# Dot products from two extra columns of a turning matmul, squares summed chunk by chunk, and one centring for both normalisations of a mixer

## The chip, the cores and the metric

The kernel runs on one core of a Trainium2 chip. A core has a matrix engine (TensorE, PE in the profile), a vector engine (VectorE, DVE), a scalar engine (ScalarE, ACT), GpSimd (POOL) and SyncE (SP, which here only issues DMAs). Each engine works through its own queue in order and waits on semaphores. The metric is the device time of one launch in microseconds (us).

## The reference

The input is 16 images of 48 channels, 64x64 pixels. Two layers, each a "mixer" and a small quantised feed-forward net, are applied with layer normalisation and residuals. The change touches the front of the second layer's mixer:

```python
center = x[:, :, H // 2, W // 2][:, :, None, None]
sim = (x * center).sum(1, keepdims=True) / (norm(center) * norm(x) + 1e-06)
x = x * (sim >= 0.7)
xd = einsum('hH,bcHW,wW->bchw', Mh, x, Mw)      # cosine transform over height and width
xt = xd.transpose(0, 2, 3, 1)
xn = (xt - xt.mean(-1)) / sqrt(xt.var(-1) + 1e-05) * ln_w + ln_b
# four quadrants of xn go through a state-space scan each; the result is added to xd,
# and the inverse transform follows
```

Before this, `x` is layer-normalised over its 48 channels: centred and scaled by 1/sqrt(var + 1e-6). So per pixel the mixer needs the sum of squares of the centred channels, their dot product with the centre pixel, a mask from both, the transform of the masked pixels, and a second normalisation over channels at each of the 64x64 frequencies.

## The kernel before

Images go in pairs: 2 x 48 channels fill 96 partitions, and the 4096 pixels lie along the free dimension. There are 8 pairs. Each engine's program is a prologue, a hardware loop over pairs 0 to 6 and a written-out last pair. At the loop's end the engine jumps back; pairs 1 to 6 begin behind such a jump, pair 0 comes straight from the prologue, pair 7 stands behind the loop.

One pair has these stages in the order of time:

- **The mixer's front.** With pixels on the 128 partitions (a "turned" tile is 32 groups of 128 pixels x 96 channels), VectorE finishes the sums of squares (line 1265) and dot products (1266), ScalarE takes logarithms and exponentials for the roots (920 to 926), VectorE forms the mask times 1/std (1271 to 1281) and scales the turned pixels (`scale(7, h)`, line 1258) in two halves. TensorE transforms columns (588, tile `pix`), turns back to rows (579), transforms rows (647); ScalarE evacuates each result from PSUM (888, 880). Then comes the second normalisation: VectorE sums channels, subtracts the mean (1252 to 1254), ScalarE squares (935), VectorE sums squares (1294), ScalarE takes ln and exp (937, 940), VectorE scales (1258 again), TensorE turns (579), ScalarE evacuates into `xq` (946).
- **The scan.** DMAs fetch `xq` back into shifted tiles, and 96 steps of multiply, scan and gather follow (lines 1323, 1328, 1417, 716, 735), with the first layer's convolution of a later pair woven in.
- **The inverse transform.**
- **The stream.** The feed-forward net of this pair, then the first net of the next pair ("ffn0"), then the normalisation ("norm") of the pair after that, chunk by chunk of 512 pixels. A norm step is: TensorE centres (538), ScalarE squares (860), TensorE averages (531), ScalarE takes ln and exp (849, 854), VectorE scales (1157) and sums (1160). Woven into the last steps is `turn_in`: for each of 8 chunks of 4 groups, TensorE turns the finished pixels of the next pair and centres them by the same matmul (514, the stationary operand is the pixels, the moving one the 96x96 matrix `centre`), and ScalarE copies the result to `pix` (836) and squares it into `pix2` (837).

The order is written by hand: `turned_in(parts, t)` says at which step t which chunk is turned. `take_centre` (1117 to 1120) picks up the centre pixel, broadcast to all partitions by a matmul with a selector (520); `sum_first_half` (1125 to 1130) multiplies the first 16 groups by it and sums both the products and the squares; GpSimd multiplies the other 16 groups (1388). `link` lets VectorE wait for its own last result. A small router for the convolution runs in the mixer's front too (1197 to 1231, TensorE 571, ScalarE 875).

Of the kernel before, what the change touches and what calls it, by code (L numbers as in the profile page):

```python
# [17 lines left out]
ALU = mybir.AluOpType  # L18
# [54 lines left out]
def program(nc, a):  # L73
# [9 lines left out]
    with ctx:  # L83

        ident = sb("ident", [128, 128])
        centre = sb("centre", [R, R])
# [40 lines left out]
        cb = sb("cb", [128, R])  # L127
        cb2 = sb("cb2", [128, R])
# [20 lines left out]
        pix2 = cut(128, GRP * R).rearrange("p (g r) -> p g r", g=GRP)  # L149
        sq = cut(R, LN_DEPTH * CH).rearrange("p (b n) -> p b n", b=LN_DEPTH)  # L150
# [52 lines left out]
        def two(b, rows=128):  # L203
# [44 lines left out]
        half_products = sem("half_products")  # L248
# [34 lines left out]
            (ident[:], "ident"), (centre[:], "centre"), (average[:], "average"),  # L283
# [28 lines left out]
        centre_ps = ps[:, 4, GB * R:(GB + 1) * R]  # L312
# [4 lines left out]
        (D_SUMS, D_MASKED, _, D_CENTRED2, _, D_VAR2, D_NORMED2, _) = range(1, 9)  # L317
        A_SQUARE = 1
        (A_LOG_V, A_LOG_S, A_RSTD, A_ROOT, A_SQUARE2, _, A_LOG2, A_RSTD2) = range(NG + 1, NG + 9)
        LN_DVE, LN_ACT = 8, NG + 8  # L320
        PROLOGUE, CHAIN = 27, 39
# [166 lines left out]
        def _(pe):  # L488
# [6 lines left out]

            def turn_in(P, n):

                c = IN_ORDER[n]
                if n == 0:
                    pe.wait_ge(hf_ready, P * 2 * NCH + NCH)  # L500
# [11 lines left out]
                for g in range(GB):  # L512
                    px = (c * GB + g) * 128
                    mm = pe.matmul(ps[:, 4 + n % 4, g * R:(g + 1) * R], x[:, px:px + 128], centre[:],
                                   start=True, stop=True)
                mm.then_inc(pix_ps, 1)
                if n == 1:

                    pe.wait_ge(ln_act, P * LN_ACT + A_SQUARE)
                    pe.matmul(centre_ps, sel_centre[:], pix[:, GRP // 2, :], start=True,  # L520
                              stop=True).then_inc(cen_ps, 1)

            def stream(n0, f0, parts, ready, src, P):

                for t in range(len(parts) + 3):
# [7 lines left out]
                    if t < len(parts):  # L533
# [4 lines left out]
                        pe.matmul(ps[0:R, j % LN_DEPTH, :], centre[:], src[parts[t]][:, j * CH:(j + 1) * CH],  # L538
# [26 lines left out]
                    if turned_in(parts, t) is not None:  # L565
                        turn_in(P, turned_in(parts, t))
# [256 lines left out]
        def _(act):  # L823
# [6 lines left out]
            chunk = lambda t, c: flat(t)[:, c * GB * R:(c + 1) * GB * R]  # L830

            def turn_in(P, n):
# [3 lines left out]
                act.activation(chunk(pix, c), ps[:, 4 + n % 4, 0:GB * R], ACT.Copy).then_inc(pix_act, 1)  # L836
                act.activation(chunk(pix2, c), ps[:, 4 + n % 4, 0:GB * R], ACT.Square).then_inc(ln_act, 1)

            def stream(n0, f0, parts, P):

                for t in range(len(parts) + 2):
# [27 lines left out]
                    if turned_in(parts, t) is not None:  # L869
                        turn_in(P, turned_in(parts, t))  # L870
# [42 lines left out]
            def pair(p, last):  # L913
# [4 lines left out]
                halves = lambda t: [flat(t)[:, h * GRP * R // 2:(h + 1) * GRP * R // 2] for h in range(2)]  # L918
# [17 lines left out]
                act.wait_ge(ln_dve, d0 + D_VAR2)  # L936
                act.activation(st[:, 2, :], st[:, 1, :], ACT.Ln, bias=eps[:, 1:2],
                               scale=1.0 / C).then_inc(ln_act, 1)
                act.wait_ge(ln_act, l0 + A_LOG2)
                act.activation(st[:, 3, :], st[:, 2, :], ACT.Exp, scale=-0.5).then_inc(ln_act, 1)  # L940
# [140 lines left out]
        def _(dve):  # L1081
# [20 lines left out]
            def link(ins):  # L1102
# [8 lines left out]
            sums_of_squares = lambda h: dve.reduce_sum(  # L1111
                nrm[:, 0, h * (ST // 2):(h + 1) * (ST // 2)], rows(half(pix2, h)), AXX)

# [448 lines left out]
```

## Time and profile before

| what | us |
|---|---|
| median of 3 runs | 4772.62 (4768.94 to 4777.07) |
| the profiled execution, its own time | 4770.02 |
| its span in the trace | 4768.1 |

| engine | busy us | share of the span |
|---|---|---|
| TensorE | 4072.2 | 85% |
| VectorE | 3633.8 | 76% |
| ScalarE | 2758.8 | 58% |
| GpSimd | 2337.8 | 49% |

The shares are means over unlike stages. In the scan nearly all engines are busy; in the mixer's front they take turns, and its time is that of the chain of waits through it. So the views below are of one pair, number 1, from the end of the stream before it (about 766 us) to the start of its scan (about 848 us).

### The profile page before, as it was taken

What the parts mean: (1) busy time and instruction counts of PE and PEld (TensorE: products, weight loads), DVE (VectorE), ACT (ScalarE), POOL (GpSimd) and SP (SyncE); (2) the same over time, 40 slices, a digit from 0 to 9 for tenths busy, and PEclk for the clock granted to TensorE, in tenths of its full rate; (3) what the DMA queues carried; (4) which work ended last, traced back from release to release, by engine and by line L of the source; (5) the groups of instructions that cost most, each with busy time, mean ns of one, the idle gap of its engine ahead of it and who ended that gap; (6) DMA issues with size and microseconds to landing.
All of it is one profiled execution on the core that took longest, in us unless ns stands there. A gap on an engine that the chain in (4) does not pass through costs nothing.

```text
span 4768.1 us, 49162 instructions
## 1 busy us (share of the span) xinstructions
PE 4072.2 (85%) x14248; PEld 1478.0 (31%) x14248; DVE 3633.8 (76%) x3157; ACT 2758.8 (58%) x3396; POOL 2337.8 (49%) x1084
## 2 busy tenths in 40 slices
PE   6779986899869998699986998779987799868997
PEld 2322233222332223322243222332233222332223
DVE  1469967699668996589965998659977699667996
ACT  2556646666566665566565664656647566565554
POOL 0137642476316773167631776227742477325663
PEclk9889988899889999799997998979999899887888
DMA  1147641577317762277623775247751576406661
GB/s 39 41 120 173 165 116 42 145 168 175 91 46 169 175 169 64 65 166 176 154 58 86 184 170 141 61 103 171 173 127 42 131 181 164 103 16 150 145 154 48
DMA packets 166829, 580.17 MB, mean 122 GB/s; under 512 B 22460, under 2 KB 23208, under 8 KB 162952
## 3 DMA queue, kind: packets, MB, share of 16 engines
q1 hardware_dynamic: 152168, 538.66, 47.4%
q10 hardware_dynamic: 14336, 37.76, 2.7%
q8 instruction: 132, 2.16, 0.2%
q14 instruction: 193, 1.58, 0.1%
HBM read 467.12 MB, written 71.48 MB: 113 GB/s over the span
## 4 chain that ended last, share of the span: by engine, by line
issue 32%; POOL 29%; PE 20%; ACT 9%; DVE 8%; DMA 1%; POOLq 0%; SPq 0%; ACTq 0%; DVEq 0%
POOL arena L1417 26%; PE ps L531 3%; PE ps L588 3%; ACT arena L867 2%; PE ps L670 2%; PE ps L579 2%; PE ps L735 2%; ACT arena L849 2%; POOL arena L1407 2%; DVE arena L1328 1%; PE ps L716 1%; PE ps L607 1%; POOL x L1425 1%; PE ps L561 1%; ACT arena L860 1%
## 5 line engine op out<-in xcount | busy, mean ns | idle before, releaser
L1417 POOL TENSOR_TENSOR arena<-arena 128x1024 f32<-128x1024 f32 x768 | 1859.6, 2421 | 972.1 <-DVE arena L1328 972.1
L1328 DVE TENSOR_TENSOR_SCAN arena<-arena,ps 128x1024 f32<-128x1024 f32 x768 | 1756.1, 2287 | 102.0 <-ACT arena L1020 4.5
L1020 ACT ACTIVATE arena<-arena,a_all 128x1024 f32<-128x1024 f32 x768 | 868.1, 1141 | 415.2 <-DVE arena L1328 277.3
L1323 DVE TENSOR_TENSOR ps<-ps,arena 128x1024 f32<-128x1024 f32 x768 | 930.7, 1212 | 159.1 <-PE ps L718 158.7
L716 PE MATMUL ps<-arena,spread 32*128 32x512 f32 x1536 | 905.0, 676 | 138.1 <-DVE arena L1328 87.3
L718 PE MATMUL ps<-arena,spread 32*128 32x512 f32 x1536 | 891.7, 676 | 0.0
L735 PE MATMUL ps<-arena,gather 128*32 128x512 f32 x3072 | 545.1, 656 | 41.2 <-POOL arena L1417 41.2
L781 PE MATMUL ps<-x 96*96 96x512 f32 x1008 | 498.5, 612 | 0.0
L716 PEld LDWEIGHTS ps<-arena,spread 32*128 32x128 f32 x1536 | 234.9, 191 | 782.0 <-issue 383.6
L670 PE MATMUL ps<-arena,w_in 96*96 96x512 f32 x512 | 322.5, 788 | 65.7 <-DMA arena<-xq 65.7
L1371 POOL TENSOR_TENSOR x<-x,arena 96x512 f32<-96x512 f32 x64 | 113.9, 1780 | 414.6 <-DVE arena L1180 414.6
L981 ACT ACTIVATE arena<-ps 128x512 f32<-128x512 f32 x128 | 76.4, 597 | 300.7 <-PE ps L702 300.7
L531 PE MATMUL ps<-arena,average 96*96 96x512 f32 x400 | 219.9, 632 | 30.8 <-ACT arena L860 30.8
L781 PEld LDWEIGHTS ps<-x 96*96 96x96 f32 x1008 | 143.1, 162 | 332.3 <-issue 332.3
L1305 DVE TENSOR_TENSOR arena<-arena 96x1024 f32<-96x1024 f32 x64 | 76.8, 1199 | 218.1 <-ACT arena L1006 218.1
L735 PEld LDWEIGHTS ps<-arena,gather 128*32 128x32 f32 x3072 | 107.9, 115 | 432.6 <-issue 354.3
L1407 POOL TENSOR_TENSOR arena<-arena 96x1024 f32<-96x1024 f32 x64 | 150.5, 2351 | 164.8 <-DVE arena L1305 164.8
L718 PEld LDWEIGHTS ps<-arena,spread 32*128 32x128 f32 x1536 | 229.8, 191 | 0.0
L1397 POOL MEMSET arena<- 96x6 f32 x8 | 0.8, 101 | 436.6 <-ACT xq L946 436.6
L849 ACT ACTIVATE arena<-ps,eps 96x512 f32<-96x512 f32 x200 | 136.4, 682 | 125.3 <-PE ps L531 125.3
L999 ACT ACTIVATE arena<-ps 96x512 f32<-96x512 f32 x128 | 70.7, 589 | 238.6 <-DVE arena L1313 226.8
L670 PEld LDWEIGHTS ps<-arena,w_in 96*96 96x96 f32 x512 | 103.3, 214 | 279.1 <-issue 210.3
(158 smaller groups left out, 5639.9 us busy)
## 6 DMA issues: line engine op xcount, KB each, us to landing
arena<-dl SPq DMA_DIRECT2D x768, 512.0 KB, 5.7
dl<-arena ACTq DMA_DIRECT2D x64, 384.0 KB, 6.2
x<-pn SPq DMA_DIRECT2D x56, 247.5 KB, 5.9
arena<-in_x SPq DMA_DIRECT2D x9, 1536.0 KB, 9.6
arena<-xq SPq DMA_DIRECT2D x64, 192.0 KB, 7.8
arena<-arena ACTq DMA_DIRECT2D x64, 192.0 KB, 5.6
out<-x SPq DMA_DIRECT2D x64, 192.0 KB, 2.1
arena<-xq SPq DMA_DIRECT2D x64, 191.8 KB, 6.7
```

Of the source, the lines that this page charges most:

```text
L531: pe.matmul(ps[0:R, LN_DEPTH + j % LN_DEPTH, :], average[:], sq[:, j % LN_DEPTH, :], start=True, stop=True).then_inc(averaged, 1)
L670: mm = pe.matmul(ps[0:DI, 6 + c, :], w_in[:, q, j, :], xs[:, i, c * 512 + 2 * j:c * 512 + 2 * j + 512], start=(j == 0), stop=(j == 1))
L716: pe.matmul(ps[:, bank, :], spread[rows[0], r, :], u[rows[0], i, 0:512], start=True, stop=True)
L718: pe.matmul(ps[:, bank + 1, :], spread[rows[1], r, :], u_low[rows[1], i, :], start=True, stop=True).then_inc(ubc_ready, 1)
L735: mm = pe.matmul(ps[b * BLK:(b + 1) * BLK, c, :], gather[:, r, :], hs[:, (r * TRIO + b) % HSS, c * 512:(c + 1) * 512], start=False, stop=( ...
L781: mm = pe.matmul(ps[0:R, 7, :], diag[:, k, :], taps_of(win[:, v % 2], k), start=(k == 0), stop=(k == TAPS - 1), skip_group_check=True)
L849: act.activation(lnv[:, k, :], ps[0:R, LN_DEPTH + k, :], ACT.Ln, bias=eps[0:R, e:e + 1]).then_inc(logged, 1)
L1020: act.activation(da[:, m % DAS, :], dbc[:, m % DBC, :], ACT.Exp, scale=a_all[:, v // 2, m:m + 1]).then_inc(da_ready, 1)
L1323: dve.tensor_tensor(driven, driven, bmat[:, v % 2, :], ALU.mult).then_inc(bu_ready, 1)
L1328: dve.tensor_tensor_scan(hs[:, m % HSS, :], da[:, m % DAS, :], driven, 0.0, ALU.mult, ALU.add).then_inc(h_ready, 1)
L1407: pool.tensor_tensor(u[:, i, :], delta, xi[:, i, :], ALU.mult).then_inc(u_ready, 1)
L1417: pool.tensor_tensor(product, product, cmat[:, v % 2, :], ALU.mult).then_inc(pr_ready, 1)
```

## The change

1. The moving matrix of the turning matmul becomes `turn_by`, 96x98: the 96 columns of `centre` and two more that hold the centred centre pixel of each image. One small matmul (`take_middle`) centres the centre pixel, and VectorE writes the two columns (`point_turn`). The dot products of all pixels then come out of the turning matmul as columns 96 and 97 of `turned`. Turning starts one step later, and ScalarE and TensorE run one step further. The products on VectorE and GpSimd and their sums go. The broadcast matmul has 2 columns in place of 96.
2. The squares are summed per chunk of 4 groups (`sum_squares`) in the stream's steps, the last chunk at the head of the pair's front.
3. The cosine transform acts on pixels, so channels that sum to zero before it sum to zero after it: the second subtraction of the mean goes. ScalarE squares the row transform straight from PSUM behind each copy; VectorE sums, and ln, exp and the scaling are done by halves.

```diff
@@ constants and tiles
-        centre = sb("centre", [R, R])
+        turn_by = sb("turn_by", [R, R + 2])
+        centre = turn_by[:, 0:R]
+        of_image = sb("of_image", [R, 2])
+        turned = cut(128, GRP * (R + 2)).rearrange("p (g r) -> p g r", g=GRP)
@@ def turned_in(parts, t):
-            return n if "ffn0" in parts and 0 <= n < NG else None
+            return n if "ffn0" in parts and 0 <= n <= NG else None
@@ TensorE
+            def take_middle(P):
+                pe.wait_ge(hf_ready, P * 2 * NCH + NCH)
+                settled(pe)
+                pe.wait_ge(ffn_done, P * 2 * NCH + MID // CH + 1)
+                pe.matmul(ps[0:R, 4, 0:2], centre, x[:, MID:MID + 2], start=True, stop=True).then_inc(centre_row, 1)
@@ def turn_in(P, n):
                 if n == 0:
-                    pe.wait_ge(hf_ready, P * 2 * NCH + NCH)
+                    pe.wait_ge(cvec_ready, P + 1)
-                    mm = pe.matmul(ps[:, 4 + n % 4, g * R:(g + 1) * R], x[:, px:px + 128], centre[:],
+                    mm = pe.matmul(ps[:, 4 + n % 4, g * TR:(g + 1) * TR], x[:, px:px + 128], turn_by[:],
-                    pe.matmul(centre_ps, sel_centre[:], pix[:, GRP // 2, :], start=True,
+                    pe.matmul(centre_ps, sel_centre[:], turned[:, GRP // 2, R:TR], start=True,
@@ ScalarE
-                evac(p, C_ROW, flat(xd[:]), 128, 512)
+                for c in range(NCR):
+                    act.wait_ge(pix_ps, p * PS_PAIR + ps_before(C_ROW) + c + 1)
+                    part = slice(c * 512, (c + 1) * 512)
+                    act.activation(flat(xd[:])[:, part], ps[:, c, :], ACT.Copy).then_inc(pix_act, 1)
+                    act.activation(flat(pix)[:, part], ps[:, c, :], ACT.Square).then_inc(ln_act, 1)
-                for h in range(2):
-                    act.wait_ge(ln_dve, d0 + D_CENTRED2 + h)
-                    act.activation(halves(pix2)[h], halves(pix)[h], ACT.Square).then_inc(ln_act, 1)
...
@@ VectorE, in the stream
+            def point_turn(P):
+                dve.wait_ge(centre_row, P + 1)
+                dve.tensor_tensor(turn_by[:, R:TR], ps[0:R, 4, 0:1].broadcast_to([R, 2]), of_image[:],
+                                  ALU.mult).then_inc(cvec_ready, 1)
+            def sum_squares(P, n):
+                c = IN_ORDER[n]
+                dve.wait_ge(ln_act, P * LN_ACT + A_SQUARE + n)
+                return dve.reduce_sum(nrm[:, 0, c * 2 * GB:(c + 1) * 2 * GB],
+                                      rows(pix2[:, c * GB:(c + 1) * GB, :]), AXX)
-                    if turned_in(parts, t) == 6:
-                        sum_first_half(P)
+                    if n == 0:
+                        point_turn(P)
+                    if n and n >= 2:
+                        sum_squares(P, n - 2)
+                    if n == 4:
+                        take_centre(P)
@@ VectorE, in the pair's front
-                dve.wait_ge(ln_act, a0 + NG)
-                sums_of_squares(1).then_inc(ln_dve, 1)
-                dve.wait_ge(half_products, (p + 1) * (NG // 2))
-                link(dve.reduce_sum(half_st(4, 1), rows(half(xd, 1)), AXX))
+                sum_squares(p, NG - 1).then_inc(ln_dve, 1)
...
-                    dve.wait_ge(pix_act, p * ACT_PAIR + act_before(C_ROW) + (h + 1) * NCR // 2)
-                    subtract_mean(xd, h)
-                for h in range(2):
-                    dve.wait_ge(ln_act, a0 + A_SQUARE2 + h)
-                    ins = dve.reduce_sum(half_st(1, h), rows(half(pix2, h)), AXX)
+                    dve.wait_ge(ln_act, a0 + A_SQUARE2 + (h + 1) * NCR // 2 - 1)
+                    dve.reduce_sum(half_st(1, h), rows(half(pix, h)), AXX).then_inc(ln_dve, 1)
                 for h in range(2):
-                    scale(3, h)
+                    dve.wait_ge(ln_act, a0 + A_LOG2 + 2 * h + 1)
+                    scale(xd[:], 3, h)
```

On VectorE, the end of the stream, the loop's jump and the head of a pair's front. Before (1157 and 1160 are a norm step's scaling and sum, 1111 a half's sum of squares, 1197 the router):

```order
L1157 TENSOR_TENSOR arena<-ps,arena 96x8x64
L1160 TENSOR_REDUCE chunk_sums<-arena 96x1
L1125 TENSOR_TENSOR xd<-arena,cb 128x1536
L1128 TENSOR_REDUCE st<-xd 128x32
L1111 TENSOR_REDUCE nrm<-arena 128x32
L1350 UNCONDITIONAL_BRANCH
L1197 TENSOR_REDUCE pooled<-chunk_sums 96x1
```

The same place after the change, where 1172 and 1175 are the norm step's two instructions and 1144 is a chunk's sum of squares:

```order
L1172 TENSOR_TENSOR arena<-ps,arena 96x8x64
L1175 TENSOR_REDUCE chunk_sums<-arena 96x1
L1144 TENSOR_REDUCE nrm<-arena 128x8 x3
L1358 UNCONDITIONAL_BRANCH
L1358 ISA
L1144 TENSOR_REDUCE nrm<-arena 128x8
L1215 TENSOR_REDUCE pooled<-chunk_sums 96x1
```

Three long instructions ahead of the jump became three short ones, and the two long ones behind it (1111 and 1266) became one short one.

On VectorE, the second normalisation before, from the end of the router (1231) to the first scaling (1258):

```order
L1231 TENSOR_TENSOR x<-ident,sel_small 96x864
L1290 ISA
L1252 TENSOR_REDUCE st<-xd 128x32
L1106 REGISTER_ALU
L1253 TENSOR_SCALAR st<-st 128x32
L1106 REGISTER_ALU
L1254 TENSOR_TENSOR arena<-xd,st 128x1536
L1290 REGISTER_ALU
L1252 TENSOR_REDUCE st<-xd 128x32
...
L1254 TENSOR_TENSOR arena<-xd,st 128x1536
L1293 REGISTER_ALU
L1294 TENSOR_REDUCE st<-arena 128x32
```

And after, where 1303 is a half's sum of squares and 1271 the scaling:

```order
L1249 TENSOR_TENSOR x<-ident,sel_small 96x864
L1302 REGISTER_ALU
L1303 TENSOR_REDUCE st<-arena 128x32
L1302 REGISTER_ALU
L1303 TENSOR_REDUCE st<-arena 128x32
L1305 REGISTER_ALU
L1271 TENSOR_TENSOR arena<-xd,st 128x1536
```

Six instructions of VectorE ahead of the sums of squares are gone. On ScalarE the six evacuations of the row transform now alternate with six squares (949 is the copy, 950 the square):

```order
L947 REGISTER_ALU
L949 ACTIVATE xd<-ps 128x512
L950 ACTIVATE arena<-ps 128x512
L947 REGISTER_ALU
L949 ACTIVATE xd<-ps 128x512
L950 ACTIVATE arena<-ps 128x512
```

Before, six copies stood there alone, and two squares of 1536 columns (935) followed them behind waits for VectorE.

## Rows read from the trace of the kernel before

**Rows 1.** Windows of pair 1: us; PE, PEld, DVE, ACT, POOL busy; PEclk; DMA; GB/s
```profile
786.00:803.00 17.00, 0.71 (x3) 0.62 (x4) 14.55 (x21) 1.47 (x6) 1.27 (x2) 0.55 0.32 102
820.00:833.00 13.00, 1.83 (x5) 0.52 (x3) 12.16 (x9) 5.36 (x7) 0.00 (x0) 0.70 0.00 0
```

**Rows 2.** Chain of waits, same pair: start us, us, what
```profile
827.27 3.42 DVE st L1294 x2
```

**Rows 3.** Timeline, VectorE, stream's end and front: start, us, what, [idle before]
```profile
785.63 0.68 DVE L1160 TENSOR_REDUCE chunk_sums<-arena 96x1 f32<-96x512 f32 x1
786.44 2.44 DVE L1125 TENSOR_TENSOR xd<-arena,cb 128x1536 f32<-128x1536 f32 x1
788.92 1.75 DVE L1128 TENSOR_REDUCE st<-xd 128x32 f32<-128x1536 f32 x1
790.79 1.75 DVE L1111 TENSOR_REDUCE nrm<-arena 128x32 f32<-128x1536 f32 x1
794.20 0.16 DVE L1197 TENSOR_REDUCE pooled<-chunk_sums 96x1 f32<-96x8 f32 x1 [1.66 <-issue]
794.58 1.74 DVE L1111 TENSOR_REDUCE nrm<-arena 128x32 f32<-128x1536 f32 x1
796.24 1.74 DVE L1266 TENSOR_REDUCE st<-xd 128x32 f32<-128x1536 f32 x1
798.58 0.23 DVE L1271 TENSOR_TENSOR nrm<-nrm 128x66 f32<-128x66 f32 x1
```

**Rows 4.** Timeline, ScalarE, same place
```profile
785.89 0.49 ACT L837 ACTIVATE arena<-ps 128x384 f32<-128x384 f32 x1
796.36 0.35 ACT L920 ACTIVATE nrm<-nrm,eps 128x66 f32<-128x66 f32 x1 [9.98 <-DVE nrm L1111]
...
796.91 0.24 ACT L926 ACTIVATE nrm<-nrm 128x66 f32<-128x66 f32 x1
```

**Rows 5.** Timeline, TensorE, same place
```profile
783.33 1.92 PE L514 MATMUL ps<-centre,x 96*128 96x96 f32 x16
794.72 0.48 PE L571 MATMUL ps<-router_w,pool_lhs 96*96 96x4 f32 x2 [9.47 <-DVE pool_lhs L1198]
```

**Rows 6.** Timeline, VectorE, prologue: the router's sum behind TensorE's product
```profile
66.64 0.16 DVE L1204 TENSOR_TENSOR rt<-ps,router_b 96x4 f32<-96x4 f32 x1 [0.58 <-PE ps L571]
```

**Rows 7.** Timeline, GpSimd, stream's end
```profile
785.32 1.95 POOL L1388 TENSOR_TENSOR xd<-arena,cb 128x384 f32<-128x384 f32 x2 [1.52 <-ACT arena L836]
```

**Rows 8.** Timeline, one norm step of the stream: TensorE, ScalarE, VectorE
```profile
779.38 1.10 PE L531 MATMUL ps<-arena,average 96*96 96x512 f32 x2 [0.19 <-ACT arena L860]
...
780.51 0.68 ACT L849 ACTIVATE arena<-ps,eps 96x512 f32<-96x512 f32 x1 [0.42 <-PE ps L531]
781.89 0.69 DVE L1157 TENSOR_TENSOR arena<-ps,arena 96x512 f32<-96x512 f32 x1 [1.61 <-ACT arena L854]
782.39 1.10 PE L531 MATMUL ps<-arena,average 96*96 96x512 f32 x2 [0.19 <-ACT arena L860]
```

**Rows 9.** Timeline, ScalarE, the row transform's evacuation
```profile
817.57 0.60 ACT L880 ACTIVATE xd<-ps 128x512 f32<-128x512 f32 x1
818.43 0.60 ACT L880 ACTIVATE xd<-ps 128x512 f32<-128x512 f32 x1 [0.26 <-PE ps L647]
```

**Rows 10.** Timeline, VectorE, the second normalisation
```profile
819.92 1.75 DVE L1252 TENSOR_REDUCE st<-xd 128x32 f32<-128x1536 f32 x1 [9.57 <-ACT xd L880]
827.27 3.40 DVE L1294 TENSOR_REDUCE st<-arena 128x32 f32<-128x1536 f32 x2
831.38 3.43 DVE L1258 TENSOR_TENSOR arena<-arena,st 128x1536 f32<-128x1536 f32 x2 [0.70 <-ACT st L940]
```

**Rows 11.** The first instruction after the front, GpSimd: min/median/max ns, first and last start
```profile
L1397 POOL MEMSET arena<- x8: 101/101/102, 262.5 to 4283.6; 96x6 f32 x8
```

**Rows 12.** The same line in windows of pairs 3 and 4
```profile
L1397 POOL MEMSET arena<- x1: 101/101/101, 1989.6 to 1989.6; 96x6 f32 x1
...
L1397 POOL MEMSET arena<- x1: 101/101/101, 2571.0 to 2571.0; 96x6 f32 x1
```

More of the change, by code:

```diff
@@ L282, in program @@
         loads = [
-            (ident[:], "ident"), (centre[:], "centre"), (average[:], "average"),
+            (ident[:], "ident"), (centre, "centre"), (of_image[:], "of_image"), (average[:], "average"),
             (pool_mask[:], "pool_mask"), (dct_t[:], "dct_t"), (dct_i[:], "dct_i"),
@@ L311, in program @@
         IN_ORDER = (NG // 2,) + tuple(c for c in range(NG) if c != NG // 2)
-        centre_ps = ps[:, 4, GB * R:(GB + 1) * R]
+        TR = R + 2
+        MID = (H // 2) * W + W // 2
+        centre_ps = ps[:, 4, GB * TR:GB * TR + 2]
         logits = ps[0:R, 2, GB * R:GB * R + E]
-        (D_SUMS, D_MASKED, _, D_CENTRED2, _, D_VAR2, D_NORMED2, _) = range(1, 9)
+        D_SUMS, D_MASKED, D_VAR2, D_NORMED2 = 1, 2, 4, 6
         A_SQUARE = 1
-        (A_LOG_V, A_LOG_S, A_RSTD, A_ROOT, A_SQUARE2, _, A_LOG2, A_RSTD2) = range(NG + 1, NG + 9)
-        LN_DVE, LN_ACT = 8, NG + 8
-        PROLOGUE, CHAIN = 27, 39
+        A_LOG_V, A_LOG_S, A_RSTD, A_ROOT = range(NG + 1, NG + 5)
+        A_SQUARE2, A_LOG2 = NG + 5, NG + 5 + NCR
+        LN_DVE, LN_ACT = 7, A_LOG2 + 3
+        PROLOGUE, CHAIN = 24, 31
         XSL = 16 * 2
@@ L537, in stream @@
                             pe.wait_ge(normed, n - LN_DEPTH + 1)
-                        pe.matmul(ps[0:R, j % LN_DEPTH, :], centre[:], src[parts[t]][:, j * CH:(j + 1) * CH],
+                        pe.matmul(ps[0:R, j % LN_DEPTH, :], centre, src[parts[t]][:, j * CH:(j + 1) * CH],
                                   start=True, stop=True).then_inc(centred, 1)
@@ L564, in stream @@
                         mm.then_inc(fc2_ready, 1)
-                    if turned_in(parts, t) is not None:
-                        turn_in(P, turned_in(parts, t))
+                    n = turned_in(parts, t)
+                    if n == 0:
+                        take_middle(P)
+                    if n:
+                        turn_in(P, n - 1)
             def router(count):
@@ L835, in turn_in @@
                 act.wait_ge(pix_ps, P * PS_PAIR + ps_before(T_IN) + n + 1)
-                act.activation(chunk(pix, c), ps[:, 4 + n % 4, 0:GB * R], ACT.Copy).then_inc(pix_act, 1)
-                act.activation(chunk(pix2, c), ps[:, 4 + n % 4, 0:GB * R], ACT.Square).then_inc(ln_act, 1)
+                bank = ps[:, 4 + n % 4, 0:GB * TR]
+                act.activation(flat(turned)[:, c * GB * TR:(c + 1) * GB * TR], bank, ACT.Copy).then_inc(pix_act, 1)
+                act.activation(pix2[:, c * GB:(c + 1) * GB, :],
+                               bank.rearrange("p (g r) -> p g r", g=GB)[:, :, 0:R],
+                               ACT.Square).then_inc(ln_act, 1)
             def stream(n0, f0, parts, P):
-                for t in range(len(parts) + 2):
+                for t in range(len(parts) + 3):
                     if 0 <= t - 1 < len(parts):
@@ L868, in stream @@
                                        ACT.Copy).then_inc(hf_ready, 1)
-                    if turned_in(parts, t) is not None:
-                        turn_in(P, turned_in(parts, t))
+                    if turned_in(parts, t):
+                        turn_in(P, turned_in(parts, t) - 1)
             def router(count):
@@ L1283, in pair @@
                 for h in range(2):
-                    scale(7, h)
+                    scale(turned[:, :, 0:R], 7, h)
                 if not last:
@@ L1468, in constants @@
         "ident": np.eye(128, dtype=np.float32),
+        "of_image": same[:, 0:R:C],
         "centre": np.eye(R, dtype=np.float32) - same / np.float32(C),
```

62 lines of the change are left out of this document (18 added, 44 removed).

## The prediction, made before the changed kernel was run

> **What bounds the kernel now.** I read four views, in this order. The windows first: in the 17 us behind the stream's end VectorE is busy for 14.55 us and TensorE for 0.71 us, and in the 13 us of the second normalisation VectorE for 12.16 and TensorE for 1.83 [rows 1]. So in these two stretches one engine works and the rest wait. The chain of waits next: it says whether that engine's work sets the end. It lies on VectorE there, with the two sums of squares of the second normalisation as one piece of 3.42 us [rows 2]. Then the timelines of VectorE and of the engines that wait for it: ScalarE has been idle for 9.98 us when it may take its first logarithm [rows 4], TensorE for 9.47 us before the router's product [rows 5]. Last the idle times inside one norm step of the stream, since the change adds work there. The step is 3.01 us long (782.39 - 779.38), and each engine has room in it: TensorE 0.19 us, ScalarE 0.42, VectorE 1.61 [rows 8]. The stream's own bound is the loop square, average, ln, exp, next square, and it stays.
>
> All of the change lies between the last norm step and the mixer's evacuation, a stretch in which nothing overlaps with another pair. Every microsecond that leaves VectorE's chain there leaves the pair's period, and there are 8 pairs.
>
> **The stream.** Turning starts one step later. In the step where it began, 8 matmul instructions (16 take 1.92 us, so about 0.9) leave TensorE's queue, and the centre pixel's product comes in, which has the form of the router's 96x4 product, 0.48 us [rows 5]. The stream ends about 0.4 us earlier. From the next step on a step holds what it held. The 98 columns in place of 96 cost 2% of 0.9 us, 0.02 us, inside TensorE's 0.19. ScalarE copies 392 columns in place of 384, 0.01 us inside 0.42. VectorE gets a sum of 384 columns in the later steps. Its price: 512 columns take 0.68 us and 1536 take 1.75 [rows 3], so 1.045 ns a column, and 384 take 0.55 us; it fits into 1.61. The centre's pick-up (three small instructions before, one now) comes one step later, ahead of the bank that the fifth turning reuses; I count nothing, since it also sheds two instructions. VectorE's small write of the two columns (about 0.2 us, by the 0.23 us of line 1271 [rows 3]) waits for TensorE's product. Behind it in VectorE's queue is only the feed-forward net's cast, which is needed a step later, so again nothing.
>
> **The end of the stream and the front's head (pair 1).** Before, the last norm sum starts at 785.63 and the root chain (line 1271) at 798.58: 12.95 us [rows 3]. In them lie 1125 (2.44), 1128, two 1111 and 1266 (1.75 each), 9.4 us of work, the router's small pieces, and 1.66 us of idle time at the loop's jump.
> After: the norm sum starts at 785.26 (0.37 earlier). The first of the three short sums follows 0.81 us behind, as 1125 did, at 786.07. They follow each other every 0.47 us (the duration less 0.08, as 1266 starts 1.66 us behind an 1111 of 1.74), so the third starts at 787.01 and ends at 787.56. ScalarE's squares keep ahead: its last one began at 785.89 [rows 4]; it has one chunk more behind the last norm step (0.75 us) and starts 0.37 earlier, so it is through by 786.8.
> Then the jump. Line 1197 starts 1.66 us behind the end of the last instruction ahead of the jump and 3.41 behind its start [rows 3]. The trace doesn't tell which counts, and short instructions hide less of it. From the end, the eighth sum starts at 789.22; from the start, at 790.42. I take the middle, 789.8, since both readings come from one row, and keep 0.6 us either way.
> Behind it: 1197 at 790.27, the router's product 0.52 us later (794.72 - 794.20) [rows 3, 5], 0.48 us long, VectorE's answer at about 791.3 (in the prologue it idled 0.58 us there, where nothing hid the product [rows 6]), and line 1271 about 0.5 us on, at 791.8. ScalarE's four roots take 0.79 us (796.36 to 797.15) [rows 4] behind the sum's end at 790.35: 791.2, so the router is now what is late, by 0.6 us. Before, it was hidden by 1111 and 1266.
> Gain: 798.58 - 791.8 = 6.8 us in the six pairs behind a jump. In pairs 0 and 7 no jump stands there: 787.48 for the eighth sum, 1271 at 789.5, against 796.8 before (798.58 less the jump's 1.75), 7.3 us. Together 6 x 6.8 + 2 x 7.3 = 55.4 us.
> From 1271 to the first scaling the same eight small instructions run; one reads two columns of `turned` with a step, 64 elements, and I count nothing.
>
> **The scaling of the turned pixels.** It reads `turned` with a row of 98 and writes `pix`, 1536 columns. Two took 3.43 us, 1.75 for the first [rows 10]. The nearest dear row is 1125, also 1536 columns with a broadcast operand: 2.44 us. That instruction began while GpSimd's product ran, until 787.27 (785.32 + 1.95) [rows 7], and 787.27 + 1.6 is its end, 788.88 [rows 3]. I take 1.75; 2.44 stays as the upper end, 0.7 us for the first half of either scaling, 1.4 us a pair, 11 us in all.
> The Trainium skill, "SBUF — State Buffer", section "SBUF: two separate sides", has it that VectorE and GpSimd share a port pair that is locked for a whole instruction, whichever starts first. By that rule the 2.44 has its cause in GpSimd, which does nothing in the new front, and the upper end falls away: 11 us less at the top of the range. This trace agrees in the one place where it can be seen.
>
> **The second normalisation.** Before: the first copy of the row transform starts at 817.57 and the copies follow every 0.86 us, paced by TensorE, with ScalarE idle for 0.26 [rows 9]. VectorE's chain runs from 819.92 to the scaling at 831.38 [rows 10], 13.81 us behind the first copy.
> After: copy and square per chunk. Back to back, copies overlap by about 0.1 us (line 837's kind is started every 0.38 us at 0.48 long; I use 0.50 for 0.60), so a chunk takes 1.0 us, more than TensorE's 0.86: ScalarE sets the pace, not TensorE. The sixth square ends 6.1 us behind the first copy, at 823.67; the third has ended at 820.67, and VectorE sums that half from there, then the other from 823.7 to 825.45. The scaling of half 0 follows at 825.4; its ln and exp (32 columns, at most 0.6 us) ran on ScalarE from 823.7 on. Gain 831.38 - 825.4 = 6.0 us. The other half's ln and exp lie beside that scaling. Bounds: 0.86 us a chunk if the squares hid wholly, 1.20 if nothing overlapped: -0.7 to +1.0 us a pair.
> 8 x 6.0 = 48 us.
>
> **Sum.** 55.4 + 48 = 103.4 us off the profiled execution's own 4770.02 us: 4666.6. The median of the runs stands 2.6 us above that execution, so 4669. One more small load among 28 at the start costs under 1 us. TensorE's clock is at its lower level for most of the front (0.55 granted [rows 1]) and I leave it so; behind shorter waits it might be higher, which I don't price.
>
> **Rivals.**
> *The jump holds the front back.* If the stretch without instructions is tied to something earlier than the last sum (the sequencer reaches the jump early, and what it waits for comes when it comes), the first instruction behind it stays at 794.20 - 0.37, so the eighth sum is 4.0 us later than in my sum, in six pairs: +24 us, 4693. The same holds if ScalarE's or TensorE's jump is longer than VectorE's; before, their 9.98 and 9.47 us of idle time hid it [rows 4, 5]. For it: 3.41 us is long for a jump. Against: VectorE's own restart lies behind its last instruction as far as can be read. Chance 0.10.
> The Trainium skill, "Runtime: NRT & Kernel Launch", section "Instruction fetch mechanics", says that a taken branch outside the fetched pages stalls the engine until the target is fetched. By this rule every engine pays at the jump, whatever work it has left, and this rival is the form it would take here. The 1.66 us agree with it; its size on ScalarE and TensorE this trace can't show.
> *ScalarE and the scalings are dearer.* At 1.20 us a chunk and 2.44 us for a scaling: +8 + 11 = +19 us, 4688. For it: line 1125. Against: line 1258 and GpSimd's row. Chance 0.08.
> *The turning outgrows its step.* This is the slower side. If a product of 98 columns, written at a step that is no multiple of 96, cost what half of a 512-column product costs (0.5 us, as the pieces of line 531 [rows 8]) in place of 0.12, a chunk's 8 pieces would take 3 us more, 2.8 beyond TensorE's room, in 8 chunks: +22.7 us a pair, +182 in all, 4851, slower by 1.6%. It decides from 103 / 64 = 1.6 us beyond the room per chunk. Nothing in the profile speaks for it. Chance 0.03.
> That the front isn't on the path after all would leave no change; the chain contradicts it. Chance 0.01.
>
> **How the numbers follow.** The forecast has 0.78. Its own range: the jump 6 x 0.6 = 4 us either way, ScalarE's pace -6 to +8, and the pairs themselves. The last differ for equal work: from pair 3 to pair 4 it is 581.4 us [rows 12], and the mean over seven is (4283.6 - 262.5) / 7 = 574.4 [rows 11]. For that I add 7 us either way. 4652 to 4688, stretched to 4691 towards the first two rivals. A measurement of this kernel tells about 0.2% (9.5 us) from no change. Faster: 0.78 + 0.10 + 0.08 = 0.96; same 0.01; slower 0.03.
>
> **What would show it.** In the changed profile: no GpSimd work between its last residual sum and the memset; three sums of 0.55 us ahead of the jump and one behind; line 1282 (the old 1271) 6 to 7 us earlier behind the last norm sum; norm steps still 3.01 us long; copy and square in pairs of 1.0 us with no wait for TensorE; the scaling some 7.8 us behind the first copy in place of 13.8; a scan as long as before. I'd be wrong if ScalarE's first logarithm waited for its own queue and not for VectorE, if the step of the stream grew, or if the scan took back what the front gives.

## The result: 78 us faster, 25 less than forecast

| | before | changed | ratio (95% interval) |
|---|---|---|---|
| median, us | 4771.73 (4768.94 to 4777.07, 4 runs) | 4694.1 (4684.73 to 4708.91, 4 runs) | 0.9839 (0.9811 to 0.9867) |
| profiled execution: own time / span, us | 4770.02 / 4768.1 | 4697.47 / 4695.7 | |

The forecast was 4669 with a range of 4652 to 4691: 25 us too low, and the measured median lies 3 us outside the range. The first rival, "the jump holds the front back", had been priced at 4693; how much that is worth is said below.

The page of the changed kernel, part 1 (busy us, share of the span, instructions):

```profile
span 4695.7 us, 49142 instructions
PE 4071.1 (87%) x14264; PEld 1475.5 (31%) x14264; DVE 3527.9 (75%) x3125; ACT 2758.9 (59%) x3444; POOL 2307.8 (49%) x1052
```

VectorE has lost 106 us of work and GpSimd 30; ScalarE and TensorE have what they had. The span fell by 72 us. So where did the path not shrink with VectorE's work? The timeline of VectorE at the front of pair 1 of the changed kernel shows it (start, us, what, [idle before]); the rows answer to [rows 3] and [rows 10]:

```profile
767.02 0.68 DVE L1175 TENSOR_REDUCE chunk_sums<-arena 96x1 f32<-96x512 f32 x1
767.82 1.47 DVE L1144 TENSOR_REDUCE nrm<-arena 128x8 f32<-128x384 f32 x3
775.64 0.55 DVE L1144 TENSOR_REDUCE nrm<-arena 128x8 f32<-128x384 f32 x1 [6.35 <-issue]
...
777.14 0.16 DVE L1222 TENSOR_TENSOR rt<-ps,router_b 96x4 f32<-96x4 f32 x1 [0.57 <-PE ps L586]
777.62 0.23 DVE L1282 TENSOR_TENSOR nrm<-nrm 128x66 f32<-128x66 f32 x1
...
780.20 3.43 DVE L1271 TENSOR_TENSOR arena<-arena,st 128x1536 f32<-128x1536 f32 x2
...
799.46 1.75 DVE L1303 TENSOR_REDUCE st<-arena 128x32 f32<-128x1536 f32 x1 [9.86 <-ACT arena L950]
...
804.06 3.42 DVE L1271 TENSOR_TENSOR arena<-xd,st 128x1536 f32<-128x1536 f32 x2
```

In this stretch one number is far from the forecast. The three short sums end at 769.29, the loop's jump follows, and VectorE's next instruction starts at 775.64: 6.35 us with nothing to do, where [rows 3] had 1.66. "issue" means that the engine waited for nothing that the profile shows. The chain of waits has the same hole on the path (start, us, what):

```profile
769.29 6.24 issue
```

ScalarE and TensorE wait for VectorE over this time, as in [rows 4, 5], and TensorE's norm step is still 3.02 us long (763.78 - 760.76, [rows 8]):

```profile
776.23 0.35 ACT L935 ACTIVATE nrm<-nrm,eps 128x66 f32<-128x66 f32 x1 [7.69 <-DVE nrm L1144]
```

```profile
760.76 1.10 PE L543 MATMUL ps<-arena,average 96*96 96x512 f32 x2 [0.19 <-ACT arena L876]
...
763.78 1.10 PE L543 MATMUL ps<-arena,average 96*96 96x512 f32 x2 [0.19 <-ACT arena L876]
...
776.62 0.48 PE L586 MATMUL ps<-router_w,pool_lhs 96*96 96x4 f32 x2 [9.09 <-DVE pool_lhs L1216]
```

What else begins at 767? The queue of SyncE (start, us to issue, what):

```profile
767.01 0.31 SPq L458 DMA_DIRECT2D pn<-arena  x1
```

This is the store of the normalised image, 1.6 MB. It waits for the scaling of the last norm step (line 1172, the semaphore `normed`), and so goes out as the last norm sum begins. The view of DMA by queue tells what the DMA engines did in the first 5 us behind the jump, and in the 3 us after that (queue, kind: packets, MB, share of the 16 engines):

```profile
DMA packets 86, 1.34 MB, mean 268 GB/s; under 512 B 9, under 2 KB 9, under 8 KB 9
q1 hardware_dynamic: 86, 1.34, 85.2%
```

```profile
q1 hardware_dynamic: 10, 0.05, 4.7%
q14 instruction: 4, 0.03, 3.3%
q8 instruction: 1, 0.02, 1.9%
```

From 768.2 to 773.2 only the store's packets move. Packets of the kind "instruction" come between 773.2 and 776.2, when the store has all but drained, and VectorE restarts then. I read them as the code behind the jump; the experiments below test that. Before, the store was issued at 785.62 and the jump, by the trace's record of the branch, came at 790.89. (A branch's record lies ahead of the end of the work already handed over: here the long sum ran on to 792.54.) The store, then the DMA queues from 790.9 to 792.0 and from 792.0 to 794.2:

```profile
785.62 0.31 SPq L453 DMA_DIRECT2D pn<-arena  x1
```

```profile
q1 hardware_dynamic: 18, 0.17, 42.1%
```

```profile
q1 hardware_dynamic: 7, 0.03, 3.9%
q8 instruction: 1, 0.02, 2.6%
q14 instruction: 2, 0.02, 2.0%
```

So only 0.20 MB of the store was left at the jump, and the first of the two packets of queue 14 started 1.2 us behind it. Now the jump comes at 768.13, 1.1 us behind the store, and the first such packet 5.3 us behind the jump.

Added up over the eight pairs of the two profiled executions, in us from start to start (the root chain begins with line 1271, now 1282; the first copy is that of the row transform, the second scaling that of the second normalisation):

| stretch | before | changed | difference | forecast |
|---|---|---|---|---|
| last scan to last norm sum (7) | 867.0 | 864.3 | -2.7 | -2.6 (0.37 each) |
| last norm sum to root chain | 99.9 | 72.0 | -27.9 | -52.4 |
| root chain to first copy of the row transform | 149.1 | 151.7 | +2.6 | 0 |
| first copy to second scaling | 110.4 | 61.5 | -48.9 | -48 |
| second scaling to first scan | 333.8 | 335.6 | +1.8 | 0 |
| the scans | 2921.1 | 2921.3 | +0.2 | 0 |

The start up to the first norm sum took 2.0 us more and the end behind the last scan 0.4, which with the rows makes the 72.4 us of the span. In the second row the six pairs behind a jump went from 12.9 to 13.3 us to 10.6 to 11.0; pairs 0 and 7, with no jump there, from 11.1 and 10.3 to 3.9 and 3.6.

### The profile page after: what moved, and what is told of

The parts are those of the page before. It is cut to its first block, busy times and chain, and to the rows that moved or that the text cites. A ratio compares the mean times of both kernels' runs of the same rounds, so it can differ in the third digit from the quotient of the medians.

```text
span 4695.7 us, 49142 instructions
## 1 busy us (share of the span) xinstructions
PE 4071.1 (87%) x14264; PEld 1475.5 (31%) x14264; DVE 3527.9 (75%) x3125; ACT 2758.9 (59%) x3444; POOL 2307.8 (49%) x1052
## 4 chain that ended last, share of the span: by engine, by line
issue 33%; POOL 30%; PE 18%; ACT 10%; DVE 7%; DMA 1%; POOLq 1%; SPq 0%; ACTq 0%; DVEq 0%
POOL arena L1416 27%; PE ps L543 3%; PE ps L603 3%; DVE arena L1336 2%; ACT arena L883 2%; ACT arena L865 2%; PE ps L594 2%; POOL arena L1406 2%; PE ps L750 2%; PE ps L685 1%; PE ps L622 1%; POOL x L1424 1%; ACT arena L876 1%; PE ps L731 1%; PE ps L573 1%
## 5 line engine op out<-in xcount | busy, mean ns | idle before, releaser
L685 PE MATMUL ps<-arena,w_in 96*96 96x512 f32 x512 | 311.9, 765 | 68.1 <-DMA arena<-xq 68.1
```

Of the source, the lines that this page charges most:

```text
L685: mm = pe.matmul(ps[0:DI, 6 + c, :], w_in[:, q, j, :], xs[:, i, c * 512 + 2 * j:c * 512 + 2 * j + 512], start=(j == 0), stop=(j == 1))
```

## The experiments

The kernel before ran on the chip beside each group of runs: 4766.57 us beside e1 to e4, 4766.54 beside e5 to e8, 4765.24 beside e9 and e10.

Theory A: the code behind the jump is fetched by the same DMA engines as the store, and waits for the store's packets that are already in flight. The rivals are given with each run.

**The store later.** In the changed kernel the store waits until ScalarE has written the logarithms, which come behind the jump:

```diff
                     sync.dma_start(a["xsp"], x[:]).then_inc(x_spilled, 16)
+                    sync.wait_ge(ln_act, p * LN_ACT + A_LOG_V)
+                    settled(sync)
                     sync.wait_ge(normed, p * LN_PAIR + LN_FIRST)
                     sync.dma_start(a["pn"], padded).then_inc(pn_out, 16)
```

> The changed kernel, with the store of the normalised image (pn, 1.6 MB) issued behind ScalarE's first logarithm of the pair's front, so behind the loop's jump, and no longer right behind the last norm step. Theory A (the instructions of the loop's head are fetched by DMA, and that fetch stands behind the store): VectorE's idle time at the jump falls from 6.35 us to 1 to 2 us, the norm sum to root chain (lines 1175 to 1282) from 10.6 to 5.5 to 6.5 us in six pairs, 26 to 30 us in all: about 4665 us. Theory B (the restart is tied to something earlier in VectorE's own queue, or the jump costs a fixed time): the idle time stays at 6.3 us, about 4694 us.

Measured: 4666.51 us (4662.93 to 4679.3, 5 runs), ratio 0.9795 (0.9769 to 0.9821). VectorE of this run, the store, and the DMA queues from 768.2 to 772.2:

```profile
767.10 0.68 DVE L1177 TENSOR_REDUCE chunk_sums<-arena 96x1 f32<-96x512 f32 x1
...
771.35 0.55 DVE L1146 TENSOR_REDUCE nrm<-arena 128x8 f32<-128x384 f32 x1 [1.97 <-issue]
```

```profile
772.44 0.31 SPq L460 DMA_DIRECT2D pn<-arena  x1
```

```profile
q14 instruction: 4, 0.03, 3.0%
q8 instruction: 1, 0.02, 2.0%
```

The code now comes at once, the idle time is 1.75 to 1.97 us, and from the last norm sum to the root chain it takes 6.0 to 6.2 us; the sum over the pairs is 44.1 for 72.0. 28 us came back with one wait, more than the 24.5 us that this row lacked of the forecast, and with them the total is within 3 us of the forecast's 4669. Theory B (a fixed time, or one tied to VectorE's own queue) falls: nothing of VectorE's changed. The store in front of the jump is the whole of what the forecast missed.

**The same wait in the kernel before.**

> The kernel before with the same later store. Theory A: its idle time of 1.66 us at the jump falls below 1 us, since the long sum ahead of the jump hides most of an undisturbed fetch: 4 to 9 us in all, about 4765 us. Theory B: 1.66 us and 4772 us.

Measured: 4769.9 us (4759.73 to 4775.48, 10 runs), ratio 1.0003 (0.9988 to 1.0017). The idle time at the jump fell from 1.65 to 2.03 us to 1.20 to 1.49:

```profile
787.99 0.16 DVE L1199 TENSOR_REDUCE pooled<-chunk_sums 96x1 f32<-96x8 f32 x1 [1.27 <-issue]
```

That is 2.4 us in all, less than the 4 to 9 us of the expectation, and the idle time did not fall below 1 us; in the total nothing is seen. The long work before the jump had given the store time to drain. So the store cost 0.4 us a pair before and 4.6 us after, in the six pairs behind a jump: the change made it dear by making VectorE early.

**A second store behind the first.** The changed kernel, and the same 1.6 MB once more to a buffer that nobody reads:

```diff
                     sync.dma_start(a["pn"], padded).then_inc(pn_out, 16)
+                    sync.dma_start(a["pn2"], padded).then_inc(pn_out, 16)
```

> The changed kernel with a second store of the same 1.6 MB, to another tensor, right behind the first. Theory A: the fetch waits for both, some 6 us more at each of six jumps (12 us idle in place of 6.35), about 4730 us. Theory B: 4694 us and 6.3 us.

Measured: 4690.63 us (4683.0 to 4707.74, 4 runs), ratio 0.9853 (0.9821 to 0.9885): not slower than the changed kernel. The jump, and the DMA queues from 772 to 779:

```profile
774.94 0.55 DVE L1145 TENSOR_REDUCE nrm<-arena 128x8 f32<-128x384 f32 x1 [6.99 <-issue]
```

```profile
q1 hardware_dynamic: 104, 1.45, 62.8%
q14 instruction: 4, 0.03, 1.2%
q8 instruction: 1, 0.02, 0.9%
```

The 5 us before that, from 767 to 772:

```profile
q1 hardware_dynamic: 101, 1.60, 103.2%
```

The expectation fell. The fetch comes some 5 us behind the jump as in the changed kernel, while 1.45 MB of the stores are still to move. By then 1.60 MB had moved, which is one store: the fetch goes in where the first store's bytes end, and not behind all bytes that are queued.

**Half a store in front of the jump.** Channels 0 to 47 at the old place, the others behind the logarithms:

```diff
-                    sync.dma_start(a["pn"], padded).then_inc(pn_out, 16)
+                    sync.dma_start(a["pn"][0:C], padded[0:C]).then_inc(pn_out, 16)
+                    sync.wait_ge(ln_act, p * LN_ACT + A_LOG_V)
+                    sync.dma_start(a["pn"][C:R], padded[C:R]).then_inc(pn_out, 16)
```

> The changed kernel with the store of the normalised image (1.6 MB a pair) in two halves: channels 0 to 47 at the old place, channels 48 to 95 only when ScalarE has written the logarithms of the same pair. Theory A (VectorE's jump waits until the packets of the store that are already handed over have drained): half the bytes are ahead of the fetch, so the idle time at the jump falls from 6.35 us to 3 to 4 us in each of the six pairs, which is about 16 us of the total: 4678 us (4670 to 4685). Rival (any store in flight costs the fetch the same wait, as the second store of e3_double_store added nothing): idle stays 6.2 to 6.5 us, 4694 us.

Measured: 4696.52 us (4677.2 to 4726.57, 4 runs), ratio 0.985 (0.9809 to 0.9892). Idle time at the jump 5.62 to 6.45 us for 6.35 to 6.75:

```profile
776.03 0.55 DVE L1146 TENSOR_REDUCE nrm<-arena 128x8 f32<-128x384 f32 x1 [5.79 <-issue]
```

The DMA queues from 769.2 to 772.4, and from 772.4 to 774.4:

```profile
q1 hardware_dynamic: 31, 0.47, 71.5%
```

```profile
q1 hardware_dynamic: 17, 0.09, 19.2%
q8 instruction: 1, 0.02, 2.9%
q14 instruction: 2, 0.02, 2.2%
```

Half the bytes saved 0.5 us a pair, not half the wait: neither the 3 to 4 us of theory A nor the 6.2 to 6.5 us of its rival was met, and the total shows nothing. In the 3.2 us of the first view the half moved at 147 GB/s (the whole at 268 in its 5 us), so it took nearly as long, and again the fetch comes where its packets run out. In these runs the wait goes by the time until the last packets of the first store, not by its bytes; why the half moves at a lower rate, and in what order a DMA engine takes the queues, they don't show.

**Only the jump moved.** The changed kernel, store as it was, with VectorE's loop boundary moved: the front's head of the next pair is written at the end of the loop's body, so that the jump lies ahead of the router's choice, where VectorE has nothing urgent to do:

```diff
-            with dve.Fori(0, PAIRS - 1) as p:
-                pair(p, False)
-            pair(PAIRS - 1, True)
+            parts(0, False)[0]()
+            with dve.Fori(0, PAIRS - 2) as p:
+                parts(p, False)[1]()
+                parts(p + 1, False)[0]()
+            parts(PAIRS - 2, False)[1]()
+            parts(PAIRS - 1, True)[0]()
+            parts(PAIRS - 1, True)[1]()
```

> The changed kernel with only VectorE's loop boundary moved, the store at its old place. Theory A (every engine's fetch waits behind the store's packets): ScalarE's and TensorE's jumps, which stand at the same place, now end last; the root chain comes 1 to 2 us earlier than in the changed kernel at most: 4686 us (4680 to 4692). Rival (only the fetch for VectorE waits behind the store): norm sum to root chain 3.9 to 4.4 us, 4655 us.

Measured: 4689.87 us (4682.09 to 4711.55, 4 runs), ratio 0.9842 (0.981 to 0.9874). VectorE's hole is gone, and ScalarE, whose jump stands where it stood, has one of its own; VectorE then waits for ScalarE:

```profile
778.66 0.51 ACT L851 ACTIVATE arena<-ps 128x384 f32<-128x384 f32 x1
785.76 0.35 ACT L935 ACTIVATE nrm<-nrm,eps 128x66 f32<-128x66 f32 x1 [6.59 <-issue]
```

```profile
786.59 0.23 DVE L1282 TENSOR_TENSOR nrm<-nrm 128x66 f32<-128x66 f32 x1 [4.74 <-ACT nrm L941]
```

The last norm sum to the root chain takes 8.9 to 9.0 us, 1.7 less than in the changed kernel, as theory A had it. ScalarE's fetch waits behind the store as VectorE's did; in the changed kernel VectorE's hole of 6.35 us had hidden ScalarE's. The row of the norm sum gives 10.7 us (61.3 for 72.0), of which the medians show 4 at most: in the profiled execution the stretch from the second scaling to the first scan took 350.2 us for 335.6, with 45 to 46 us in four pairs where the others have 42. What that is, these runs don't show. Theory A in its wording goes one step further than the runs: the profile counts both kinds of packets on the core's 16 DMA engines, and that they wait for each other there is the reading that fits all of these runs; the records have no engine for a packet.

**Both.** The jump moved and the store behind the logarithms:

> e1_late_store with VectorE's loop boundary moved from behind the norm's last sum but one to the place ahead of the router's choice, where VectorE has been idle for 9.9 us in any case. Theory A (the jump costs what the fetch costs, wherever it stands, and is free where the engine idles longer): norm sum to root chain falls from 6.0 to 3.9 to 4.4 us in six pairs, so 10 to 12 us less than e1_late_store: 4655 us (4650 to 4660). Rival (ScalarE's and TensorE's own jumps end as late as VectorE's and take its place): norm to root stays at 5.5 to 6 us, 4664 us or more.

Measured: 4652.58 us (4634.08 to 4668.02, 6 runs), ratio 0.9755 (0.973 to 0.978). VectorE and ScalarE:

```profile
777.88 0.68 DVE L1177 TENSOR_REDUCE chunk_sums<-arena 96x1 f32<-96x512 f32 x1
778.68 1.93 DVE L1146 TENSOR_REDUCE nrm<-arena 128x8 f32<-128x384 f32 x4
...
782.03 0.23 DVE L1284 TENSOR_TENSOR nrm<-nrm 128x66 f32<-128x66 f32 x1
...
790.30 0.15 DVE L1231 TENSOR_REDUCE rs<-rt 96x1 f32<-96x4 f32 x1 [2.46 <-issue]
```

```profile
781.14 0.35 ACT L937 ACTIVATE nrm<-nrm,eps 128x66 f32<-128x66 f32 x1 [1.74 <-DVE nrm L1146]
```

The four sums run on without a break, the jump's 2.46 us lie where nobody waits for VectorE, and the last norm sum to the root chain takes 4.15 us here (782.03 - 777.88) and 4.2 in every pair with a jump; the sum over the eight pairs is 32.4 for 44.1. The expectation of 3.9 to 4.4 us and 4655 us is met. This is the best version: 2.45% below the kernel before, where the change alone reaches 1.61%.

**The second normalisation alone.** The kernel before, with this part of the change:

```diff
-                evac(p, C_ROW, flat(xd[:]), 128, 512)
+                for c in range(NCR):
+                    act.wait_ge(pix_ps, p * PS_PAIR + ps_before(C_ROW) + c + 1)
+                    part = slice(c * 512, (c + 1) * 512)
+                    act.activation(flat(xd[:])[:, part], ps[:, c, :], ACT.Copy).then_inc(pix_act, 1)
+                    act.activation(flat(pix)[:, part], ps[:, c, :], ACT.Square).then_inc(ln_act, 1)
...
-                    dve.wait_ge(pix_act, p * ACT_PAIR + act_before(C_ROW) + (h + 1) * NCR // 2)
-                    subtract_mean(xd, h)
...
-                    scale(3, h)
+                    dve.wait_ge(ln_act, a0 + A_LOG2 + 2 * h + 1)
+                    scale(3, h, xd[:])
```

> The kernel before with part 3 of the change alone (no second subtraction of the mean, squares from PSUM behind each copy, ln, exp and scaling by halves); dot products and sums of squares as before. Both theories: the stretch from the first copy of the row transform to the scaling falls from 13.80 to 7.7 us in every pair, 8 x 6.1 = 49 us, about 4723 us; the jump's idle time stays at 1.66 us. If it moved less, the scan takes part of it back.

Measured: 4742.16 us (4727.03 to 4745.63, 6 runs), ratio 0.9939 (0.9918 to 0.9961). From the first copy to the second scaling it takes 7.7 us for 13.8 in all eight pairs, the full 48.9 us, but the scans took 25 us more than before (2946.1 for 2921.1), and the median is 19 us above the 4723 expected.

**The other part alone.** The changed kernel with the second normalisation as before:

> The changed kernel with the second normalisation as it was before (copy, subtraction of the mean, and the sums after it); the norm's squares by chunk and the shared front stay changed. If the two parts add up: norm sum to root chain 10.6 to 11 us in the six pairs with a jump, first copy to second scaling 13.8 us in all eight, 4772 - 28 = 4744 us. Rival (each part alone gives some 20 us back in the scans through TensorE's lower clock, as the second normalisation alone did): the scans sum to over 2940 us and the total is 4760 us or more.

Measured: 4751.66 us (4741.72 to 4762.54, 10 runs), ratio 0.9968 (0.9956 to 0.9981). The profiled execution took 4741.72 us and holds what was expected of the head: norm sum to root chain 10.6 to 11.0 us in six pairs. Its scans took 2915.7 us, so the rival's 2940 didn't come. The median is 8 us above the expectation. The two parts alone give 24 and 15 us where both together give 78, so either they help each other or something of the runs' own is in these numbers. Two more runs looked at that, each part with the store behind the logarithms.

> The kernel before with the change of the second normalisation alone (as e4_second_norm_alone) and the store of the normalised image behind ScalarE's logarithms. The question is the 25 us that the scans of e4_second_norm_alone took more than those of before. If that was the clock of one execution (chance): the scans sum to 2915 to 2930 us, copy to second scaling 7.7 us a pair, 4767 - 49 - 2 = 4716 us (4708 to 4724). If the second normalisation without the rest of the change lengthens the scans by itself: they sum to 2940 us or more, 4735 us or more.

Measured: 4709.67 us (4699.81 to 4728.89, 4 runs), ratio 0.9888 (0.984 to 0.9935). The scans in windows, one for each of pairs 0 to 2, first of e4_second_norm_alone, then of this run (us, VectorE busy (instructions), granted clock, DMA share, GB/s):

```profile
289.00:660.00 371.00, 343.63 (x205) 0.94 0.67 163
864.00:1226.00 362.00, 342.87 (x205) 0.97 0.71 167
1428.00:1802.00 374.00, 344.17 (x206) 0.94 0.68 162
```

```profile
288.00:651.00 363.00, 343.08 (x205) 0.96 0.69 167
855.00:1218.00 363.00, 343.09 (x205) 0.97 0.70 167
1421.00:1784.00 363.00, 343.06 (x205) 0.97 0.70 167
```

The same scan with the same VectorE work takes 371 to 374 us at a granted clock of 0.94 and 362 to 363 at 0.96 to 0.97. Over the eight it is 2898 us here and 2946 there, though both kernels have the changed second normalisation. So the changed second normalisation doesn't lengthen the scans by itself. The length goes with the granted clock of the execution, 48 us between these two; that the clock is the cause is argued from this, not tested. The later store alone didn't shorten the scans elsewhere: 2921.4 us for 2921.1 in the kernel before, 2920.5 for 2921.3 in the changed one. The expectation had put the scans at 2915 to 2930 us, so they came out shorter than either of its cases, and the total (4708 to 4724) was met in part by that.

> The changed kernel with the second normalisation as before (as e6_first_part_alone) and the store behind ScalarE's logarithms. If the store in front of the jump is the whole of what the prediction missed in the head: norm sum to root chain 6.0 to 6.2 us in six pairs, so 55 us less than before by the head alone, 4767 - 55 = 4712 us (4705 to 4722). If some other cost of the shared front took the place: 4735 us or more.

Measured: 4711.97 us (4696.81 to 4726.73, 5 runs), ratio 0.9903 (0.9869 to 0.9936). The expectation was 4712. Norm sum to root chain took 6.0 to 6.1 us. With the store out of the way the parts alone give 56 and 53 us (4765.24 less 4709.67 and 4711.97), both together 100 (4766.57 - 4666.51). They add up to 109, within the scatter of the scans. Why e4 and e6 fell short stays open. e4's profile shows the slower scans at the lower clock, but its six times (4727 to 4746) and those of e9_second_norm_late_store (4700 to 4729) hardly meet, and the later store explains 3 of the 32 us between the medians (norm sum to root chain 96.8 us for 99.9). Between e6 and e10_first_part_late_store it explains 28 of 40 us. So it may be more than the scatter of single executions, and no run tells what.

## Why the prediction was wrong

The step that failed is **the jump**: "I take the middle, 789.8, since both readings come from one row, and keep 0.6 us either way." The prediction weighed two readings of one gap, 1.66 us behind the end of the last instruction and 3.41 behind its start, and both had the gap go with VectorE's own work. The range of 0.6 us was half the distance between them, not the distance to other causes. In the changed kernel the gap is 6.35 to 6.75 us. The eighth sum starts 8.62 us behind the norm sum (775.64 - 767.02), where the sum had 4.5 (789.8 - 785.26). That is 4.1 us in six pairs, 24.5 us, and 4669 + 24.5 = 4693.5 stands against 4694.1 measured.

What stood in the profile and wasn't read is SyncE's queue. The prediction has no line on the store that goes out as the last norm sum begins, since the change doesn't touch it: its price was put at nothing. It went out 5.3 us ahead of the jump's record before and 1.1 us ahead of it now, and there it costs 4.6 us a pair.

The rival **the jump holds the front back** came true in its number (4693) and in its first form: VectorE's restart is tied to something other than its last instruction. It had left the restart where it was, 8.57 us behind the norm sum (794.20 - 0.37 - 785.26), and the changed kernel has 8.62. That the two agree is luck: before, the restart followed a long sum that ended at 792.54, now it follows the store. It is no property of the jump: with the store later the restart comes 4.25 us behind the norm sum (771.35 - 767.10, by the start of that sum in e1_late_store). Its second form, a jump of ScalarE that takes over, is what e8_jump_moved_early_store shows. The rule of the Trainium skill, "Runtime: NRT & Kernel Launch", section "Instruction fetch mechanics", that a taken branch can stall an engine until its target is fetched, agrees with every run here: with the DMA engines free the stall showed as 1.75 to 1.97 us on VectorE, behind the store as 6.35 to 6.75. A chance of 0.10 was low for a stall that a named rule described and that had 3.41 us of unexplained time to its credit.

The other steps, each against its measurement:
- **The stream.** Forecast 0.4 us earlier (the 0.37 that the sum uses is not worked out there), norm steps of 3.01 us. Measured 0.39 a pair (2.7 over seven) and 3.02. The 98-column products cost nothing that can be seen; the rival of 4851 us is out.
- **The head without a jump.** For pairs 0 and 7 the sum has 4.2 us (789.5 - 785.26) from norm sum to root chain, measured 3.9 and 3.6. Behind an undisturbed jump it has 6.5 and e1_late_store shows 6.0 to 6.2. So the short sums, the router's product with its 0.57 us of idle time and the root's order were right, and slightly dear: 3.4 us over the eight pairs (55.8 us gained there in e1_late_store, 52.4 forecast).
- **The scaling of the turned pixels.** 1.75 taken for each, 3.43 us for two measured. The upper end of 2.44 falls away, and GpSimd does nothing there. The Trainium skill's rule on the shared port pair ("SBUF — State Buffer", section "SBUF: two separate sides") agrees again, but no run here puts GpSimd back to test it.
- **The second normalisation.** Forecast 48 us, measured 48.9. A pair of copy and square was put at 1.0 us, and it takes 0.96 to 0.97, with ScalarE never waiting for TensorE:

```profile
796.38 0.60 ACT L949 ACTIVATE xd<-ps 128x512 f32<-128x512 f32 x1
796.87 0.59 ACT L950 ACTIVATE arena<-ps 128x512 f32<-128x512 f32 x1
797.35 0.60 ACT L949 ACTIVATE xd<-ps 128x512 f32<-128x512 f32 x1
```

  The scaling starts 7.68 us behind the first copy (804.06 - 796.38), where the forecast had 7.8.
- **The scan takes nothing back.** 2921.3 us for 2921.1.

## What to carry to other kernels

In this kernel the code behind a loop's jump came only when the store issued ahead of it had all but drained. So look at what SyncE issues in the microseconds ahead of a jump, and move either the large transfer behind the jump or the jump to where its engine idles anyway, on every engine that waits there. When a change makes an engine early, ask which transfers that were over before will now be in flight beside it. And an idle time in the profile that no engine ends ("issue") is to be explained before it is carried over into a sum; where two readings of it are possible, a third is too.

## What the runs showed of the hardware

- The packets of the kind "instruction" at a jump came only where the packets of the store ahead of it ran out, and the engine restarted behind them. By the start of the first such packet of queue 14 in pair 1, counted from VectorE's jump: 0.5 us with the store later, 1.2 in the kernel before, 5.3 in the changed kernel. VectorE's restart followed it by 2.7, 2.1 and 2.2 us. Behind 1.6 MB issued 1.1 us ahead of the jump VectorE stood idle for 6.35 to 6.75 us, without it for 1.75 to 1.97; ScalarE for 6.59 to 6.69 with the same store.
- A second store of 1.6 MB queued right behind the first added 1.2 us over all eight pairs (73.2 for 72.0 from norm sum to root chain); half of the store in front of the jump saved 0.5 us a pair. So the wait went neither by the bytes queued nor by the bytes of the store.
- The scan of equal work took 362 to 374 us at a granted clock of 0.97 to 0.94, in the windows above. Executions of one kernel differ by 10 us and more (4684.73 to 4708.91 for the changed one).
